# Zero-tile products, the order of the pre-activations and the gate-bias rows in a two-layer AdaLN / GRU kernel

## The reference

```python
x = x + L0_ffn(L0_cond(x, u, u, cond))         # u: (16, 128, 16), cond: (16, 128)
x = x + L1_ffn(L1_cond(x, h0=cond))

L0_cond:  y = x @ W.T + fc_bias + (x @ v / 128) @ u.T / 16 + b ; gelu(y)      # v = u, per sequence
L0_ffn:   Wq = clip(round(W / (mean|W| + 1e-5)), -1, 1) for W1 and W2
          relu(x @ Wq1.T + b1) @ Wq2.T + b2                                   # hidden width 512
L1_cond:  GRU over 128 steps, for all 16 sequences at once
          Z = sigmoid(Xz + H @ Whz.T + bhz);  R = sigmoid(Xr + H @ Whr.T + bhr)
          Ht = tanh(Xh + (R * H) @ Whh.T + bhh);  H = Z * H + (1 - Z) * Ht;  Y = H @ Whq.T + bhq
          with Xz = x @ Wxz.T + bxz and so on
L1_ffn:   router argmax over 32 experts, a 128 -> 32 -> 128 MLP of the chosen expert per token
```

## Time and profile before

| | us |
|---|---|
| median of 3 runs | 282.23 |
| lowest and highest | 281.21 and 283.01 |
| the profiled execution | 281.78 |
| its span from first to last instruction | 280.0 |
| busy in the span: TensorE products, VectorE, ScalarE, GpSimd | 241.8, 230.5, 130.4, 15.1 |

### The profile page before, as it was taken

How to read it: one execution, slowest core, us unless ns; L and a number is a source line. 1 busy time by engine, 2 the same in 40 slices (tenths; PEclk the granted TensorE clock), 3 DMA queues, 4 the chain that set the end, 5 groups by cost and what they waited for, 6 DMA issues and landing times.

```text
span 280.0 us, 8338 instructions
## 1 busy us (share of the span) xinstructions
PE 241.8 (86%) x2834; PEld 171.9 (61%) x2834; DVE 230.5 (82%) x1551; ACT 130.4 (47%) x695; POOL 15.1 (5%) x19
## 2 busy tenths in 40 slices
PE   6987866889998998889898998899888998698896
PEld 6964644666665665566565665566566665465675
DVE  5874889888988988898979888898979887878873
ACT  1165545355435644465436544465436543344432
POOL 2593000000000000000000000000000000000000
PEclk9999555555898569955997579955996599869759
DMA  6940000000000000000000000000000000000000
GB/s 147 354 168 4 1 2 1 3 1 4 2 1 22 0 4 2 19 5 2 0 4 19 2 5 0 22 2 0 4 20 2 4 0 2 22 1 4 0 21 19
DMA packets 3465, 6.25 MB, mean 22 GB/s; under 512 B 757, under 2 KB 2189, under 8 KB 3296
## 3 DMA queue, kind: packets, MB, share of 16 engines
q1 hardware_dynamic: 2576, 3.91, 4.3%
q10 hardware_dynamic: 768, 1.72, 1.9%
q0 software_dynamic: 80, 0.11, 0.1%
HBM read 4.68 MB, written 1.05 MB: 20 GB/s over the span
## 4 chain that ended last, share of the span: by engine, by line
PE 50%; DVE 25%; ACT 9%; issue 7%; POOL 5%; DMA 3%; POOLq 0%
PE ZH L919 8%; PE R L919 6%; PE R L918 6%; DVE m_p L738 5%; PE ZH L918 5%; DVE rh_p L706 5%; ACT R L393 5%; ACT ZH L418 4%; PE O L804 3%; DMA const_sb<-consts 3%; PE F L859 2%; DVE rh_p L711 2%; PE F L786 2%; PE F L787 2%; PE F L788 2%
## 5 line engine op out<-in xcount | busy, mean ns | idle before, releaser
L393 ACT ACTIVATE R<-R 128x16 f32<-128x16 f32 x128 | 21.5, 168 | 67.9 <-PE R L919 67.9
L418 ACT ACTIVATE ZH<-ZH 128x16 f32<-128x16 f32 x128 | 21.5, 168 | 57.6 <-PE ZH L919 57.1
L919 PE MATMUL R<-m_p,gru_hi 128*128 128x16 f16 x256 | 46.0, 180 | 0.0
L919 PE MATMUL ZH<-rh_p,gru_hi 128*128 128x16 f16 x256 | 43.0, 181 | 1.3
L919 PE MATMUL ZH<-m_p,gru_hi 128*128 128x16 f16 x256 | 38.0, 172 | 0.0
L918 PEld LDWEIGHTS ZH<-rh_p,gru_lo 128*128 128x128 f16 x128 | 13.1, 102 | 39.0 <-DVE rh_p L706 35.0
L918 PE MATMUL ZH<-rh_p,gru_lo 128*128 128x16 f16 x128 | 23.3, 182 | 13.9 <-DVE rh_p L706 5.8
L738 DVE TENSOR_TENSOR m_p<-keep,ZH 128x16 f16<-128x16 f32 x128 | 21.7, 170 | 14.8 <-ACT ZH L418 13.7
L919 PEld LDWEIGHTS ZH<-rh_p,gru_hi 128*128 128x128 f16 x256 | 26.1, 106 | 12.2 <-DVE rh_p L711 0.2
L706 DVE TENSOR_TENSOR rh_p<-R,hist 128x16 f16<-128x16 f32 x128 | 22.3, 174 | 12.1 <-ACT R L393 5.5
L918 PE MATMUL R<-m_p,gru_lo 128*128 128x16 f16 x128 | 23.6, 184 | 7.5 <-DVE m_p L738 0.7
(11 more groups left out here) (242 smaller groups left out, 768.2 us busy)
## 6 DMA issues: line engine op xcount, KB each, us to landing
x_sb<-xT SPq DMA_DIRECT2D x4, 256.0 KB, 8.1
xs_sb<-xsT SPq DMA_DIRECT2D x1, 1024.0 KB, 11.6
outT<-res SPq DMA_DIRECT2D x7, 128.0 KB, 1.9
ffn_sb<-ffn ACTq DMA_DIRECT2D x1, 512.0 KB, 6.4
w_sb<-w ACTq DMA_DIRECT2D x1, 512.0 KB, 11.0
w_sb<-w SPq DMA_DIRECT2D x1, 512.0 KB, 10.7
gru_sb<-gru ACTq DMA_DIRECT2D x1, 448.0 KB, 9.6
expand_sb<-expand ACTq DMA_DIRECT2D x1, 128.0 KB, 9.8
```

The lines of the kernel that those rows point to most:

```text
L393: nc.scalar.activation(r_io, r_io, ACT.Sigmoid).then_inc(r_made, 1)
L418: nc.scalar.activation(c_io, c_io, ACT.Tanh).then_inc(cand_made, 1)
L919: return mm(out, gru_hi[:, WHR + gate, :], part, start=False, stop=low, skip_group_check=True)
```

## The change

TensorE gets 26 products of a zeroed 128x128 float16 tile, `idle`, ahead of the low-rank products; they wait only for the memset of that tile, which is now VectorE's first. All five pre-products go ahead of gamma's product on TensorE. On VectorE the four effective weights come in a row, `pre_activations(0)` goes ahead of the magnitude sums, `(1)` and `(2)` follow them, `(3)` stands between the comparisons and `ternary(0)`, and `(4)` between the two ternaries. The gate biases come as rows of a [128, 384] array: rows 0 and 1 hold the two biases of each gate, rows 32 and 33 hold them again, and the rest is zero. GpSimd casts the whole tile to float16 and then replaces rows 32 to 63 by what the cast lost. The wait for the consts moves from GpSimd to VectorE's step 3, and the memset of `gbias` goes.

```diff
-NZ = 6
+WARM_UP = 26
+NZ = 5
...
-        gb_sb = sb("gb_sb", [3, 2, GATES, C])
+        gb_sb = sb("gb_sb", [128, GATES * C])
+        idle = sb("idle", [128, 128], F16)
-        ones16 = sb("ones16", [128, N], BF16)
+        ones16 = sb("ones16", [128, N], F16)
-        gbias = sb("gbias", [128, GATES * C], BF16)
+        gbias = sb("gbias", [128, GATES * C], F16)
...
             pool.wait_ge(gb_in, 16)
-            pool.wait_ge(const_in, 16)
-            t_t(gsum[:], flat[:, 0, :], flat[:, 1, :], ALU.add).then_inc(gb_step, 1)
...
-            t_t(gbias[0:3, :], gpick[:, 2, :], gpick[:, 3, :], ALU.add).then_inc(gb_step, 1)
+            t_s(gbias[:], gb_sb[:], 0.0, None, ALU.add).then_inc(gb_step, 1)
+            pool.wait_ge(gb_step, 1)
+            t_t(gbias[32:64, :], gb_sb[32:64, :], gbias[32:64, :], ALU.subtract).then_inc(gb_step, 1)
+            pool.wait_ge(gb_step, 2)
...
-            for tile in (gbias, pen, mask, pen_last, mask_last, expand_off):
+            nc.vector.memset(idle[:], 0.0).then_inc(idle_set, 1)
+            for tile in (pen, mask, pen_last, mask_last, expand_off):
...
             dve.wait_ge(early_in, 16)
-            effective_weights(0)
-            effective_weights(1)
-
+            for i in range(4):
+                effective_weights(i)
+            dve.wait_ge(bias_made, 1)
+            pre_activations(0)
             dve.wait_ge(ffn_in, 16)
             nc.vector.tensor_reduce(asum[:], ffn_sb[:], AX.X, ALU.add,
                                     apply_absolute_value=True).then_inc(asum_made, 1)
-            effective_weights(2)
-            effective_weights(3)
+            pre_activations(1)
+            pre_activations(2)
             dve.wait_ge(gamma_mm, 1)
...
-            dve.wait_ge(bias_made, 1)
             below_threshold(0)
             below_threshold(1)
-            pre_activations(0)
+            pre_activations(3)
             ternary(0)
-            for i in range(1, len(PRE_GROUPS)):
-                pre_activations(i)
+            pre_activations(4)
             ternary(1)
...
                 if t == 3:
+                    dve.wait_ge(const_in, 16)
...
+            def warm_up(passes):
+                for _ in range(passes):
+                    mm(O_bank[:, 0:128], idle[:], idle[:], start=True, stop=True)
+
+            pe.wait_ge(idle_set, 1)
+            warm_up(WARM_UP)
             pe.wait_ge(v_first_in, 16)
             low_rank(0)
...
+            for i in range(len(PRE_GROUPS)):
+                pre_product(i)
             pe.wait_ge(asum_made, 1)
             pe.wait_ge(ones_set, 2)
             mm(F_bank[0][:, 0:2], ones[:], asum[:], start=True, stop=True).then_inc(gamma_mm, 1)
-            for i in range(len(PRE_GROUPS)):
-                pre_product(i)
...
-            pe.wait_ge(gb_step, 10)
+            pe.wait_ge(gb_step, 2)
```

More of the change, by code:

```diff
@@ L84, in build @@
         gru_sb = sb("gru_sb", [128, 7, C])
-        gb_sb = sb("gb_sb", [3, 2, GATES, C])
-        const_sb = sb("const_sb", [128, 128 + 2 * E + 3])
+        gb_sb = sb("gb_sb", [128, GATES * C])
+        const_sb = sb("const_sb", [128, 128 + 2 * E])
         expand_sb = sb("expand_sb", [E, NE * 128])
@@ L191, in build @@
             ("gb_in", "const_in", "expand_in", "router_in", "w1_in", "w2_in", "b1_in", "b2_in"))
-        ones_set, zeros_set, pen_ones = sem("ones_set"), sem("zeros_set"), sem("pen_ones")
+        idle_set, ones_set, zeros_set, pen_ones = sem("idle_set"), sem("ones_set"), sem("zeros_set"), sem("pen_ones")
         vv_mm, weff_made, pre_mm, pre_made, g_made = (sem(n) for n in
@@ L265, in _ @@
             nc.gpsimd.memset(ones16[:], 1.0).then_inc(ones_set, 1)
+            t_t, t_s = nc.gpsimd.tensor_tensor, nc.gpsimd.tensor_scalar
             pool.wait_ge(gb_in, 16)
-            pool.wait_ge(const_in, 16)
-            flat = gb_sb[:].rearrange("p s g c -> p s (g c)")
-            pick = const_sb[:, 128 + 2 * E:128 + 2 * E + 3]
-            t_t, t_s = nc.gpsimd.tensor_tensor, nc.gpsimd.tensor_scalar
-            t_t(gsum[:], flat[:, 0, :], flat[:, 1, :], ALU.add).then_inc(gb_step, 1)
+            t_s(gbias[:], gb_sb[:], 0.0, None, ALU.add).then_inc(gb_step, 1)
             pool.wait_ge(gb_step, 1)
-            t_s(gpart[:, 0, :], gsum[:], 0.0, None, ALU.add).then_inc(gb_step, 1)
+            t_t(gbias[32:64, :], gb_sb[32:64, :], gbias[32:64, :], ALU.subtract).then_inc(gb_step, 1)
             pool.wait_ge(gb_step, 2)
[L278 to L289, removed]
-            t_t(gbias[0:3, :], gpick[:, 2, :], gpick[:, 3, :], ALU.add).then_inc(gb_step, 1)
             pool.wait_ge(g_hi_made, 1)
@@ L1101 @@
     f32 = np.float32
+    gates = np.zeros((128, GATES * C), f32)
+    for top in (0, 32):
+        gates[top] = np.concatenate([a(L1_cond_bxr), a(L1_cond_bxz), a(L1_cond_bxh)])
+        gates[top + 1] = np.concatenate([a(L1_cond_bhr), a(L1_cond_bhz), a(L1_cond_bhh)])
     rows = [a(L0_cond_fc_bias)[None], a(cond_1024), a(L0_ffn_b1).reshape(NF, 128), a(L0_ffn_b2)[None],
@@ L1113 @@
                                           L1_cond_Whz, L1_cond_Whh, L1_cond_Whq)], 1),
-        "gate_bias": np.stack([np.stack([np.stack([a(L1_cond_bxr), a(L1_cond_bxz), a(L1_cond_bxh)]),
-                                         np.stack([a(L1_cond_bhr), a(L1_cond_bhz), a(L1_cond_bhh)])])] * 3),
-        "consts": np.concatenate([np.eye(128, dtype=f32), np.tile(np.arange(E, dtype=f32), (128, 2)),
-                                  np.eye(128, 3, dtype=f32)], 1),
+        "gate_bias": gates,
+        "consts": np.concatenate([np.eye(128, dtype=f32), np.tile(np.arange(E, dtype=f32), (128, 2))], 1),
         "expand": np.repeat(np.eye(E, dtype=f32), HE, axis=1),
```

## The result

The changed kernel takes 283.93 us (median of 10 runs, 282.93 to 285.60), the kernel before 282.06 us in its 10 runs (281.21 to 283.01). The ratio is 1.0073, 95% interval 1.0048 to 1.0097: slower by 0.7%, under the 1% that was to be told apart, but clear of zero. The forecast was 284.0 us.

The account below looks back on a forecast made before the run. The recurrence was taken as the bound, movable only by the stretch before step 0. First hidden product +2.35 us (15.6 + 4.88 - 0.5 = 20.0, not 17.64), bias products -0.1: 281.78 + 2.25 = 284.0 us, range 279.8 to 287.3.

Parts of the forecast that it names:

- part 1: 26 zero products lead TensorE from 1.1 to 4.1 us; low-rank products end at 11.1 (clock low) or 7.6 (clock risen).
- Part 2: Pre-products ahead of gamma still wait for x, whose fourth quarter lands at 14.15 us; they end at 15.6, before 15.58.
- P: End of the pre-products on TensorE, taken as 15.6 us, against 15.58 before.
- rival C: Zero products only delay, clock rises late, pre-products end at 18.1 us: +2.5 on the forecast, 286.5 us; chance 0.17.
- Part 3: Stretch from last pre-product to first hidden product, now holding gamma, thresholds, comparisons and first ternary: 4.88 us, before 2.06.
- Part 4: GpSimd does two operations for ten: biases cost nothing, and VectorE, beside a silent GpSimd, gains 0.5 us.
- The 0.1 us for the bias products: Ahead of step 0: bias products no longer wait for GpSimd's chain and move ahead of x1, gaining 0.1 us.
- The sum: First hidden product at 20.0 us instead of 17.64, +2.35; bias products -0.1; 281.78 + 2.25 = 284.0 us.
- Rival D: FFN stage runs at 1.2 GHz because TensorE idles after gamma and before the first hidden product: 288.3 us; chance 0.13.
- Rival B: Faster: x's fourth quarter lands before 12.4 us; with landing at 10.5, first hidden product 15.8, time 279.8 us; chance 0.12.
- The recurrence passed the shift on: In the 128 recurrent steps: they hardly depend on the clock, so a shift of their start moves the end one for one.

## Why the prediction was right, and where it was only lucky

The forecast time, sign and size stand: +2.25 us forecast, +1.87 between the medians. But two terms of the sum were off in opposite ways.

*The lower end of part 1 was right.* The zero products run from 0.97 to 3.9 us and the low-rank products end at 11.0, predicted 11.1 for a clock that stays low. In neither of the two profiles of the changed kernel did the clock rise before 16 us.

*Part 2 mis-sized P.* I took 15.6; the profiles have 17.55 and 17.22. The step that failed is "what starts early is lost again on a transfer". The last quarter of x was issued at 3.1 us and the slowest quarter took 10.2, so all of x was there by 13.3 us and not at 14.15, in spite of 183 KB more, and no pre-product waited for it: TensorE was still at the low clock with the second group. What the early start lost, it lost to the clock, which rose only near 17.0 us in the one profile and near 16.3 in the other. The working had a slip here too. With the first two groups done at 14.6 and the clock risen by then, the last 16 passes take 16 x 0.111 = 1.8 us, which makes P 16.4, and not 16.0. So by its own prices a low-rank stage at the low clock already led past 15.6, and the zero products, which the sum put at nothing, had a price. The profiles lie between these slow bounds, 16.4 and 18.1, two thirds or more of the way from 15.6 to rival C's 18.1, and I gave C 0.17. The transfer does bound P when the clock is up, as the 64-product kernel shows.

*Part 3 had the mechanism, and was 0.66 us too dear.* 4.88 - 0.5 = 4.38 us was forecast for gamma to first hidden product; it took 3.72. The terms that were off are gamma to gam, 0.31 instead of 0.72 (gamma's two passes took 0.28 us at the high clock and 0.59 at the low, and in the kernel before VectorE was still busy with the effective weights), and the instructions behind the comparisons, 2.06 (19.21 to 21.27) instead of 2.31, since they overlap. The comparisons took 1.35 us from gam, against 1.85 - 0.52 = 1.33. With gamma in the middle and the last pre-activation ahead of the first ternary it was 2.04, as before, which shows that this chain is what the order costs behind P.

*Part 4, the gain on VectorE, was right and too small.* Forecast 0.5 us, shown 2.23 - 1.35 = 0.88 us, in two profiles whose kernels differ in the gate biases. It only pays in the new order, where VectorE's thresholds are on the path; in the old it brings the first hidden product no closer to P (2.06 us in both). The prediction left out the nthr of 0.15 us that ran beside gpart, a row against its reading; that kernels with a silent GpSimd had no slow thr, nthr or comparison is what bears it out. The 0.1 us for the bias products didn't come.

*The sum.* Against before's profiled execution: P +1.97, behind it 3.72 - 2.06 = +1.66, together the 3.63 us by which the first hidden product is late; forecast were +0.02 and +2.32. That is 1.3 us more than forecast, and the profiled execution took 285.1 us where 284.0 was forecast. The median agrees with 284.0 since that execution was among the slower of the ten. The median span of the ten is 282.15 us; less the 255.9 behind the first sigmoid, that puts the sigmoid at 26.25 where 26.0 was forecast, and P, 6.12 + 3.72 us earlier, at 16.4. This is an estimate, and the spread of 255.6 to 256.9 makes it 15.4 to 16.7. If it holds, P was 0.8 us later than forecast and the chain behind it 0.66 us shorter, and the two cancelled: that the time came out so close is luck. By ratios the shares are: order with new biases +0.8 us, zero products on top of it +0.7 to +1.3 us, biases alone nothing. In my sum the order was the whole loss and the zero products cost nothing, so the split was wrong where the total was right.

*Rival D* didn't come: the clock stayed up from 17.1 to 30.7 us, and the FFN stage took as long as before. *Rival B* fell twice: x was there by 13.3 us, and B needed it before 12.4; and with the clock up for all pre-products, in the kernel with 64 zero products, P was 14.90 and the first hidden product still came at 18.62, behind 17.64. The recurrence passed the shift on, as forecast.

What stays open: how often the 26 zero products raise the clock. Of four profiles of kernels that have them ahead of 16-row products, one shows it; with full-height products behind them the one profile does too (low-rank passes of 0.127 us from 3.74 on). And how P is spread over the executions that were only timed, about which the two profiles of the changed kernel, both slower than its median, say little.

## What to carry to other kernels

Before work is led early, look at which clock it will run and what stands behind the last piece: here an early start was paid in low-clock passes, and a product of two columns, queued behind the last big one, with the thresholds and comparisons that hang on it, put 1.7 us in front of the last gelu. Warm the clock with the work itself where it can be had (zero rows under products that are needed anyway came with a gain of 1.4 us; 26 extra products cost 0.7 to 1.3 us in the new order, and in the old some 0.35, which isn't clear of zero), and look at more than one profile: one in four told another story, and P differed by a microsecond between two kernels with the same work ahead of it. A quiet GpSimd is worth something only where VectorE is on the path.

## What the runs showed of the hardware that was not expected

- Zeros and ones raise TensorE's clock alike: 64 products took 5.73 and 5.79 us, with the spacing halved inside. Products on 16 rows, dense for seven microseconds, didn't raise it in any profile (passes of 0.22 us up to gamma or the first pre-product); with 112 zero rows added the same passes did, near 9 us (the first 16 took 3.77 us and the second 3.09).
- Once up, the clock stayed up through 3.8 us of 16-row products in the profile with 64 zero products, and fell during them in the one with 26 (0.50 from 7.6 us), with TensorE busy up to 8.0.
- VectorE is slower beside a busy GpSimd: two comparisons of 128x512 took 0.88 us with GpSimd silent and, with it at work, 1.44 in the kernel with the order alone and 1.12 in the kernel before.
- GpSimd took 0.90 us for 384 elements on 32 partitions and as much on 3.
